# A two-layer gated decoder: the second layer transposes the low 16 bits of its fp32 rounding words

## The reference, cut to what matters

```python
x = x + tanh(g_xattn[0]) * L0_xattn(layernorm(x), ctx, ctx)      # layer 1: sigmoid attention
x = x + tanh(g_ffn[0])   * L0_ffn(layernorm(x), ...)             # layer 1: routed feed-forward
x = x + tanh(g_xattn[1]) * L1_xattn(layernorm(x), ctx, mask, ...)# layer 2: softmax attention, 16 heads
x = x + tanh(g_ffn[1])   * L1_ffn(layernorm(x), W1, W2)          # layer 2: 512 -> 2048 -> 512
```

```python
def _dyn_quant(x):                      # before wq and before wo
    s = maximum(max(abs(x), axis=-1) / 127.0, EPS)
    return clip(round(x / s), -127, 127), s
def _act_quant(x):                      # before W1 and before W2
    scale = 127.0 / clip(max(abs(x), axis=-1), 1e-05)
    xq = clip(round(x * scale), -128, 127) / scale
h = silu(_bitlinear(x, W1)); return _bitlinear(h, W2)   # W1, W2 rounded to -1, 0, 1
```

## Time and profile before

| | |
|---|---|
| time, median of 3 runs | 1096.93 us (1096.7 to 1097.64) |
| profiled execution, its span | 1095.9 us |
| PE busy | 948.6 us, 87% |
| DVE busy | 785.2 us, 72% |
| ACT busy | 555.7 us, 51% |
| POOL busy | 91.9 us, 8% |
| mean granted TensorE clock | 0.953 of 2.4 GHz |

### The profile page before, as it was taken

One profiled execution on the slowest core, in us unless ns is written; L12 is line 12 of the kernel. 1 busy time (PEld: TensorE's weight loads), 2 busy tenths in 40 slices (PEclk: granted clock), 3 DMA queues, 4 the chain that ended last, 5 costly groups with the idle time before them and its releaser, 6 DMA issues.

```text
span 1095.9 us, 17834 instructions
## 1 busy us (share of the span) xinstructions
PE 948.6 (87%) x5776; PEld 614.5 (56%) x5784; DVE 785.2 (72%) x1975; ACT 555.7 (51%) x1106; POOL 91.9 (8%) x68
## 2 busy tenths in 40 slices
PE   3899889999999987479998989998899898899557
PEld 2777666777777554256643556544466544566224
DVE  5878863443615069479798789798699798799565
ACT  3544321222221157279834579636489637599233
POOL 4444100000000000000021000040000040000100
PEclk9999989999999998689999999999989999999769
DMA  6331400100103086850019520129510148300001
GB/s 214 113 115 39 154 1 1 52 25 12 64 0 115 1 314 209 169 135 2 5 48 206 130 79 2 40 53 187 147 40 2 40 95 189 102 2 2 1 0 39
DMA packets 45898, 86.06 MB, mean 79 GB/s; under 512 B 7409, under 2 KB 7409, under 8 KB 44785
## 3 DMA queue, kind: packets, MB, share of 16 engines
q1 hardware_dynamic: 42448, 80.24, 26.4%
q0 software_dynamic: 576, 4.19, 1.0%
q10 hardware_dynamic: 2784, 0.54, 0.3%
HBM read 43.01 MB, written 8.39 MB: 47 GB/s over the span
## 4 chain that ended last, share of the span: by engine, by line
PE 32%; DVE 14%; issue 7%; SPq 5%; DMA 4%; ACT 2%; DVEq 0%; POOL 0%; POOLq 0%; ACTq 0%
PE psum L1304 9%; PE psum L1321 7%; PE psum L1279 6%; SPq L959 4%; PE psum L1373 3%; PE psum L1347 3%; DMA k<-k_lo 3%; DVE h_amax L1643 1%; PE psum L1330 1%; DVE amax L1524 1%; DVE xn L1508 1%; DVE stats L49 1%; DMA x_in<-x_mid_dram 1%; DVE hact L1654 1%; SPq L970 1%
## 5 line engine op out<-in xcount | busy, mean ns | idle before, releaser
L1106 ACT ACTIVATE probs<-psum,neg_max 128x512 f32<-128x512 f32 x256 | 174.6, 690 | 31.4 <-DVE neg_max L1586 30.5
L1586 DVE CUSTOM_DVE_ANT_0 psum<-psum,m_in 128x512 f32<-128x512 f32 x256 | 174.8, 701 | 10.4 <-issue 7.8
L1304 PE MATMUL psum<-ident,probs 128*128 128x128 f32 x1024 | 157.4, 278 | 0.0
L1304 PEld LDWEIGHTS psum<-ident,probs 128*128 128x128 f32 x1024 | 129.9, 143 | 21.9 <-issue 5.1
L1279 PE MATMUL psum<-k,q 128*128 128x512 f32 x256 | 127.1, 502 | 16.3 <-ACT probs L1106 12.3
L496 PE MATMUL psum<-w_sb,hT 128*128 128x512 f32 x256 | 115.0, 592 | 0.0
L380 ACT ACTIVATE hT<-psum,b_col 128x256 f32<-128x256 f32 x64 | 26.9, 470 | 134.6 <-PE psum L416 134.6
L937 POOL TENSOR_TENSOR xres<-xres,xn 128x512 f32<-128x512 f32 x16 | 19.9, 1271 | 860.0 <-DVE xn L1697 859.9
L1612 DVE COPY probsT<-psum 128x512 f32<-128x512 f32 x128 | 87.9, 687 | 2.6 <-PE psum L1304 2.5
L1097 ACT COPY probsT<-psum 128x512 f32<-128x512 f32 x128 | 74.9, 585 | 22.6 <-PE psum L1304 20.5
L414 PE MATMUL psum<-xselT_hi,w_hi 128*128 128x256 f32 x256 | 82.2, 321 | 4.1 <-ACT onehotT L374 4.1
(11 more groups left out here) (209 smaller groups left out, 1733.8 us busy)
## 6 DMA issues: line engine op xcount, KB each, us to landing
c_in<-in_ctx_dram SPq DMA_DIRECT2D x8, 1024.0 KB, 5.2
bw_in<-in_L_ffn_W_dram SPq DMA_DIRECT2D x8, 1024.0 KB, 11.6
k<-k_hi SPq DMA_DIRECT2D x32, 256.0 KB, 7.1
k<-k_lo SPq DMA_DIRECT2D x32, 256.0 KB, 8.3
q<-q_hi SPq DMA_DIRECT2D x64, 128.0 KB, 2.4
q<-q_lo SPq DMA_DIRECT2D x64, 128.0 KB, 2.3
xres<-in_x_dram SPq DMA_DIRECT2D x4, 1024.0 KB, 5.2
w_raw<-in_L_ffn_w_dram POOLq DMA_DIRECT2D x4, 1024.0 KB, 5.1
```

Source lines behind the costliest of these rows:

```text
L1106: act.activation(probs[:, u % 4, :], psum[u % SCORE_BANKS][:, :], ACT.Exp, scale=-1.0, bias=neg_max[:, u:u + 1], accum_out=prob_sum[:, nt, ...
L1304: mm = pe.transpose(turn_bank(u)[:, l * P:(l + 1) * P], probs[:, u % 4, l * P:(l + 1) * P], ident[:, :])
L1586: dve.tensor_tensor_reduce(bank[:, :], bank[:, :], m_in[:, nt, :], -1.0, LOWEST, ALU.add, ALU.min, neg_max[:, u:u + 1]).then_inc(masked_re ...
```

## The change

The first rounding pass now adds `TURN` = 1.5 * 2^23 + 2^14 instead of `ROUND`. The low 16 bits of each fp32 word then hold 2^14 + q, with q the rounded value. The second pass is gone. TensorE's transposes read these low 16 bits as bf16 numbers with a step of two (4 bytes), straight from the fp32 buffer (`xn`, `xnq` or `hact`). In PSUM the 16 bits are read as an int16, and the copy out subtracts 2^14 and writes bf16: on ScalarE as an Identity activation with a bias column, on VectorE as a `tensor_scalar`.

`qx`, `qxq` and `hq` are gone, `hact` has three buffers, and so its reuse for t = 3 waits for the transposes of t = 0. GpSimd only adds the residual. `hq_ready` is signalled by `round_hidden` for t = 0, 1 and 3, and TensorE waits for ScalarE's `h_rounding` for t = 2. On VectorE `residual(b, 0)` moves behind the rounding of t = 3. The prologue's weight chunks keep their two passes.

```diff
+LOW = 2.0 ** 14
+TURN = ROUND + LOW
+def low_halves(ap):
+    return ap.bitcast(BF16)[:, 0::2]
+        sh.psum_i = [t[:, :].bitcast(I16) for t in sh.psum]
-        hact = at("hact", [P, 2, DF], F32, arena)
-        hq = at("hq", [P, 2, DF], BF16, arena + 16 * K)
+        hact = at("hact", [P, 3, DF], F32, arena)
...
@@ gpsimd
-                    if more:
-                        pool.wait_ge(xnq_rounding, b * T + T)
-                        pool.tensor_tensor(held[:, 12:13], ones[:, 0:1], ones[:, 0:1], ALU.add)
-                        for t in range(T):
-                            pool.tensor_scalar(qxq[:, t, :], xnq[:, t, :], -ROUND, None, ALU.add).then_inc(qxq_ready, 1)
@@ scalar, turned_rows
-                        act.copy(qxT[:, 2 * i:2 * i + 2, :], psum_b[i][:, :]).then_inc(qxT_ready, 1)
+                        act.activation(qxT[:, 2 * i:2 * i + 2, :], psum_i[i][:, :], ACT.Identity,
+                                       bias=low_col[:, 0:1]).then_inc(qxT_ready, 1)
@@ scalar, hidden
-                        if t >= 2 and f == 0:
-                            act.wait_ge(hq_ready, b * T + t - 1)
+                        if t == 3 and f == 0:
+                            act.wait_ge(hqT_psum, b * T * 2 + 2)
@@ scalar, hidden_turned
-                        act.copy(hqT[:, t % 2, 8 * i:8 * i + 8, :], psum_b[i][:, :]).then_inc(hqT_act_ready, 1)
+                        act.activation(hqT[:, t % 2, 8 * i:8 * i + 8, :], psum_i[i][:, :], ACT.Identity,
+                                       bias=low_col[:, 0:1]).then_inc(hqT_act_ready, 1)
@@ tensor, turn_rows and turn_hidden
-                                              qx[:, t, c * P:(c + 1) * P], ident_b[:, :])
+                                              low_halves(rounded[:, t, c * P:(c + 1) * P]), ident_b[:, :])
-                    pe.wait_ge(hq_ready, b * T + t + 1)
+                    if t == 2:
+                        pe.wait_ge(h_rounding, b + 1)
+                    else:
+                        pe.wait_ge(hq_ready, b * (T - 1) + min(t, 2) + 1)
-                                              hq[:, t % 2, (8 * i + j) * P:(8 * i + j + 1) * P], ident_b[:, :])
+                                              low_halves(hact[:, t % 3, (8 * i + j) * P:(8 * i + j + 1) * P]),
+                                              ident_b[:, :])
@@ vector
-                def quantize(link):
+                def quantize():
                     for t in range(T):
-                        dve.tensor_scalar(xn[:, t, :], xn[:, t, :], inv[:, t:t + 1], ROUND, ALU.mult,
-                                          ALU.add).then_inc(link.sem, 1)
-                        link.count += 1
-                    link.wait()
-                    for t in range(T):
-                        dve.tensor_scalar(qx[:, t, :], xn[:, t, :], -ROUND, None, ALU.add).then_inc(qx_ready, 1)
+                        dve.tensor_scalar(xn[:, t, :], xn[:, t, :], inv[:, t:t + 1], TURN, ALU.mult,
+                                          ALU.add).then_inc(qx_ready, 1)
-                def whole_hidden(b, t, link):
-                    if t == 2:
-                        dve.wait_ge(h_rounding, b + 1)
-                    if t >= 2:
-                        dve.wait_ge(hqT_psum, (b * T + t - 1) * 2)
-                    dve.tensor_scalar(hq[:, t % 2, :], hact[:, t % 2, :], -ROUND, None, ALU.add).then_inc(hq_ready, 1)
+                def round_hidden(t):
+                    dve.tensor_scalar(hact[:, t % 3, :], hact[:, t % 3, :], h_inv[:, t:t + 1], TURN,
+                                      ALU.mult, ALU.add).then_inc(hq_ready, 1)
-                    dve.tensor_copy(hqT[:, t % 2, 8:16, :], psum_b[1][:, :]).then_inc(hqT_dve_ready, 1)
+                    dve.tensor_scalar(hqT[:, t % 2, 8:16, :], psum_i[1][:, :], -LOW, None, ALU.add).then_inc(hqT_dve_ready, 1)
```

More of the change, by code:

```diff
@@ L8 @@
 I32 = mybir.dt.int32
+I16 = mybir.dt.int16
 F32R = mybir.dt.float32r
@@ L708, in layer1 @@
     Q_SCALE = float(HD) ** -0.5
-    ident, ident_b, ones, psum, psum_b = sh.ident, sh.ident_b, sh.ones, sh.psum, sh.psum_b
+    ident, ident_b, ones, psum, psum_b, psum_i = sh.ident, sh.ident_b, sh.ones, sh.psum, sh.psum_b, sh.psum_i
     gate_x1, gate_f1 = sh.gates[:, 1:2], sh.gates[:, 3:4]
@@ L755, in layer1 @@
         round_col = sb("round_col", [P, 1])
+        turn_col = sb("turn_col", [P, 1])
+        low_col = sb("low_col", [P, 1])
         x_at = region("x_at", 8 * K)
@@ L933, in _, with batch @@
             def _(pool):
-                def batch(b, more):
+                def batch(b):
                     for t in range(T):
@@ L937, in batch @@
                         pool.tensor_tensor(xres[:, t, :], xres[:, t, :], xn[:, t, :], ALU.add).then_inc(x3_ready, 1)
-                    if more:
-                        pool.wait_ge(xnq_rounding, b * T + T)
-                        pool.tensor_tensor(held[:, 12:13], ones[:, 0:1], ones[:, 0:1], ALU.add)
-                        for t in range(T):
-                            pool.tensor_scalar(qxq[:, t, :], xnq[:, t, :], -ROUND, None, ALU.add).then_inc(qxq_ready, 1)
                 with pool.Fori(0, B - 1) as b:
-                    batch(b, True)
-                batch(B - 1, False)
+                    batch(b)
+                batch(B - 1)
             @block.sync
@@ L1076, in rounded_queries @@
                         act.activation(xnq[:, t, :], xnq[:, t, :], ACT.Identity, scale=inv_q[:, t:t + 1],
-                                       bias=round_col[:, 0:1]).then_inc(xnq_rounding, 1)
+                                       bias=turn_col[:, 0:1]).then_inc(xnq_rounding, 1)
                 def query_highs(b, q_hi):
@@ L1123, in round_hidden @@
                     act.wait_ge(h_inv_ready, b + 1)
-                    act.activation(hact[:, t % 2, :], hact[:, t % 2, :], ACT.Identity, scale=h_inv[:, t:t + 1],
-                                   bias=round_col[:, 0:1]).then_inc(h_rounding, 1)
+                    act.activation(hact[:, t % 3, :], hact[:, t % 3, :], ACT.Identity, scale=h_inv[:, t:t + 1],
+                                   bias=turn_col[:, 0:1]).then_inc(h_rounding, 1)
                 def hidden_turned(b, t, banks):
@@ L1394, in batch @@
                         pe.wait_ge(out_scaled, b * T + T)
-                        query_rows(b + 1, scale_q, qxq, qxq_ready, (b + 1) * T)
+                        query_rows(b + 1, scale_q, xnq, xnq_rounding, (b + 1) * T)
                         values(b + 1, range(T - 1, T))
@@ L1398, in batch @@
                     pe.wait_ge(qx_ready, b * 2 * T + 3 * T)
-                    turn_rows(qx)
+                    turn_rows(xn)
                     if more:
@@ L1545, in query_rows @@
                     dve.memset(held[:, 9:10], 0.0).then_inc(sx_ready, 1)
-                    quantize(link)
+                    quantize()
                 def query_stats(b, link):
@@ L1728, in batch @@
                         hidden_scales(b, t, link)
-                        round_hidden(t, link)
-                        whole_hidden(b, t, link)
+                        round_hidden(t)
+                        row_scale(t, link)
                     hidden_scales(b, 2, link)
                     hidden_scales(b, 3, link)
+                    round_hidden(3)
+                    row_scale(2, link)
+                    row_scale(3, link)
                     residual(b, 0)
-                    round_hidden(3, link)
-                    whole_hidden(b, 2, link)
-                    whole_hidden(b, 3, link)
                     hidden_turned(b, 2)
```

29 lines of the change are left out of this document (13 added, 16 removed).

## The result

The changed kernel takes 1088.18 us (median of 4 runs, 1085.6 to 1091.8) against 1097.29 us before (4 runs, 1096.7 to 1098.12): ratio 0.9921, 95% interval 0.9895 to 0.9947. Timed a second time in e5, on another occasion, it took 1089.43 against 1095.26: 0.9935, 0.9911 to 0.9959. The forecast was 1089.8. The profiled executions: span 1095.9 before, 1087.1 after, 8.8 us less. Of all executions behind this document three took over 1700 us (one of the kernel before, one of e4, one of e7); the ratios leave them out.

A forecast was written before the change was run, and what follows sets the result against it. Bound: the chain from VectorE's fourth `k_lo` through SyncE's key copies to ScalarE's first silu, then TensorE in the feed-forward. Terms -3.9 - 2.6 - 2.5 + 0.2 + 1.7 = -7.1: span 1088.8, time 1089.8 us, range 1086 to 1100.

The forecast's parts named there:

- First `quantize`, loop turns: Without VectorE's second pass the key copies start and land earlier: net -1.3 us a turn, -3.9 over three turns.
- rival B: The keys' landing does not move, as query DMAs share the engines: the -3.9 falls away, 1093.7 us; chance 0.12.
- Second `quantize`: In the loop turns TensorE's 2.25 us wait goes, but it then waits longer before up 1: gain 0.
- Feed-forward: In the loop turns the wait before turn 2 goes and turn 3's second half shortens: -0.87 us each, -2.6 together.
- Last batch: Both second passes (1.43 us each) leave the path, both pairs of copies add 0.19 each: -2.5 us.
- Prologue: The pass that goes was covered; two dearer copies push ScalarE's weight rounding back: +0.2 us.
- Copies: ScalarE's copies of turned rows with a bias operand: +0.09 us each, +0.19 for two in a row.
- VectorE's copy from int16: In the feed-forward, a `tensor_scalar` in place of a COPY: taken at 692 ns, bounds 692 and 1222 ns, 0 either way.
- Stepped loads: TensorE's transposes reading 16-bit numbers 4 bytes apart: no change taken, the other end +52 ns a transpose.
- Rival A: Transpose loads with a step of two are as slow as fp32 ones: +15.4 us, 1105.2 us; chance 0.17.
- Clock: TensorE's longer idle before up 1 lowers its clock in two of three turns instead of one: +1.7 us.
- Rival C: The clock falls in all three turns, twice as long: +8.5 instead of +1.7 us, time 1096.6; chance 0.09.

The follow-up runs named there:

- e5: The changed kernel unaltered, timed again on another occasion: 1089.43 us, ratio 0.9935.
- e4: Changed kernel with `hact`'s three slots in another order and ScalarE's wait for the key copies moved to the first silu of t = 1: 1076.19 us, 0.9801.
- e7: Changed kernel with GpSimd's rounding pass over the queries put back and the queries' transposes waiting for it: 1090.91 us, 0.9955.
- e6: Changed kernel with a VectorE pass nobody reads put back after the first `quantize`, in the loop turns alone: 1097.18 us, 1.0011.
- e3: Changed kernel with 14 more matmuls nobody reads between up 0 and up 1 in each loop turn: 1086.26 us, 0.9909.
- e9: e4's kernel with VectorE, not ScalarE, taking the second copy of turned rows before output projections and the last batch's feed-forward: 1078.24 us, 0.9834.
- e8: e4's kernel with 16 and 40 matmuls nobody reads ahead of the last batch's two waits for `qx_ready`: 1077.09 us, 0.9816.

## Why the prediction was right, point by point

- First `quantize`, loop turns, -3.9: measured -4.4 to the fourth `k_lo` and +0.7 from there to up 1, -3.7. The step is shown by e6 from the other side: the pass put back moves `k_lo` by 1.46 us a turn. The queries' overlap was charged at 0.1 a turn and cost 0.24, 0.4 more in e6: a piece of rival B. Two thirds of the 0.7 are the second turn's, where the queries had come late before (23.3 us behind `k_lo`), held up by the low clock. The 207 GB/s that the prediction gave for B are of 917 to 918 us, after the keys had landed.
- Second `quantize` 0: right. Its wait (1.62 us in the first turn, 2.25 in the other two) went into the wait before up 1, which grew from 6.5 to 10.9 us over three turns; 3.5 to 3.7 us each, inside the 3.3 to 3.8 that the prediction gave.
- Feed-forward, -2.6: measured -2.5. The 0.66 us wait is gone in the two turns that had it, which gained 1.0 each. In the third turn before, up 1 had been slowed by the low clock, so turn 2 came late and did not wait; only 0.44 was won.
- Last batch, -2.5: -2.5 to the second transposes, -2.3 to up 0; the rest (-0.9) is clock.
- Prologue +0.2: not shown. The stretch that holds it and the first attention took 144.0 us before, and 144.3 and 143.7 in the two traces of the changed kernel, so it moves by more than the term.
- Copies +0.09: 1015 to 1111 ns. The Trainium skill (ScalarE: Activation LUTs, "What ACT_TABLE_LOAD costs") gives some 93 ns for a pointer operand; the trace agrees (96 ns). The +0.19 for two in a row is less sure: the wait ahead of the output projection in the loop turns was 1.93 us before, and 1.90 in one trace and 2.12 in the other of the changed kernel.
- VectorE's copy from int16: 692 ns, the lower bound, as taken. The Trainium skill (VectorE: DVE Perf Modes, "Why PSUM operands drop a tier") caps PSUM operands at two 16-bit elements a cycle; the traces fit it (692 ns with two bytes on both sides, as the bf16 copy took, and 1222 ns written as fp8), but no run here tests the cap.
- Stepped loads, no change: 98 ns each and 16 transposes in 1.06 us, as before. Rival A is refuted.
- Clock, +1.7: mis-sized. The forecast had 3.4 us of cold quarters in the loop turns, 1.7 of them new; the traces have 4.2 and 5.7, so +2.6 and +4.0; it is the term that e3 gives back. Its basis was misread too. "One in three turns fell" counts the second turn as a wait that held, but TensorE waited only 0.80 us before up 1 there, and the low clock had come after the 2.25 us ahead of the transposes (0.56 at 746 to 748 us), where the wait for the keys covered it. Rival C came in part: in e5 all three turns fell, but lost 1.4 to 2.6 us each and not 3.4; one of six turns held through 3.66 us of idle and another lost 2.8. So a wait of this size does not bring the low clock back each time.

That the sum came out near is in part luck. The trace's -8.8 holds 2.2 of layer 1's clock and 0.9 of the last batch's; without layer 1 the two traces show -6.6 and -6.1 against the forecast's -7.1. The ends 1086.5 and 1092.5 that the prediction gives its forecast do not follow from the bounds beside them: no cold stretch more and free copies make 1087.2, and two stretches more at double length 1094.9.

What the prediction did not use is that the stretch before up 1 had become the largest thing to win: it named the DMA as cover, and not that the cover came from where `hact` lies, which the words on the kernel before had said.

## What to carry to other kernels

A wait for a DMA can be one for its source: look whether the writer that waits needs those bytes, and let the tile that comes first use bytes which no transfer reads. Work taken off an engine pays only up to the next thing that it feeds; follow it to there, and ask what the idle time does to the clock. A short instruction moved onto a loaded engine brings its wait along, and everything behind it pays that.

On the offset 2^14: by the number formats alone, 2^14 + q for q from -128 to 127 is, read as bf16, a number from 1.0 to just under 4.0, while a small negative q without the offset would be the bit pattern of a NaN. No run left the offset out.

## What was not expected of the hardware

- Same code, same inputs: layer 2's first `amax` moved by 5 us between executions, with the time that TensorE had spent at the low clock ahead of it (14 to 27 us).
- Idle stretches of 3.5 to 3.7 us cost between 0 and 2.8 us of low clock in six turns of the same kernel; 5.2 to 5.6 us (e6) cost 1.9 to 2.8 each time; 0.6 us (e3) and 1.4 to 1.8 us (e9) cost nothing in three turns each. Yet 2.17 us right behind filled work still had the low clock after it (e8), and of the three 2.25 or 1.62 us waits of the kernel before one did.
- GpSimd's elementwise pass beside VectorE stretches the latter's fp32 `tensor_scalar` of 4 x 128x512 from 1.92 to 3.27 us (e7; 3.40 in the kernel before).
